# An audio tower with routed experts on one core: streams laid out time by time, layer 4 in three blocks, and expert tiles ordered and cut by their tokens

## What is computed

```python
CONVS = [(128, 10, 5)] + [(128, 3, 2)] * 4 + [(128, 2, 2)] * 2
for w, g, b, s in zip(conv_ws, ln_gs, ln_bs, strides):
    h = gelu(layernorm_over_channels(conv1d(h, w, s), g, b))
out = layernorm(h) @ proj_w + proj_b                 # (64, 12, 192)
attn = softmax(q @ k.T * SCALE) @ v                  # 6 heads of 32, 12 tokens
route_prob = softmax(xt @ Ws + bs)                   # 768 tokens, 9 experts
p, routes = max(route_prob), argmax(route_prob)
h = gelu(xt @ W1[e] + b1[e]); out_e = h @ W2[e] + b2[e]   # 192 -> 768 -> 192
final = where(routes == 0, common * scaling, p * out_routes + (1 - p) * common)
```

## Time and profile before

| | |
|---|---|
| median of 3 runs | 563.9 us (563.47 to 564.89) |
| the profiled execution | 564.41 us, of which the page's span is 562.6 us |
| PE / PEld busy | 537.1 us (95%) / 504.7 us (90%) |
| ACT / DVE / POOL busy | 322.7 (57%) / 309.5 (55%) / 258.6 us (46%) |
| mean granted TensorE clock | 0.982 |

### The profile page before, as it was taken

One profiled execution on the slowest core, in us unless ns is written; L12 is line 12 of the kernel. 1 busy time (PEld: TensorE's weight loads), 2 busy tenths in 40 slices (PEclk: granted clock), 3 DMA queues, 4 the chain that ended last, 5 costly groups with the idle time before them and its releaser, 6 DMA issues.

```text
span 562.6 us, 11208 instructions
## 1 busy us (share of the span) xinstructions
PE 537.1 (95%) x4099; PEld 504.7 (90%) x4099; DVE 309.5 (55%) x767; ACT 322.7 (57%) x557; POOL 258.6 (46%) x298
## 2 busy tenths in 40 slices
PE   6898999999999999999999999999999997899995
PEld 6797989999999999999999999999899886799995
DVE  4665465457567666757575766654564443612231
ACT  1567657747675776677575757773663423444440
POOL 5683464785239427732863394243242120033343
PEclk9999999999999999999999999999999996799998
DMA  7490001692000100000000000000000087151110
GB/s 196 124 276 10 1 15 35 171 239 59 20 1 20 24 5 7 20 22 5 2 20 20 7 20 1 20 6 2 2 6 6 0 218 193 40 142 44 45 39 12
DMA packets 19505, 29.46 MB, mean 52 GB/s; under 512 B 2620, under 2 KB 13846, under 8 KB 19452
## 3 DMA queue, kind: packets, MB, share of 16 engines
q1 hardware_dynamic: 16140, 18.95, 12.7%
q0 software_dynamic: 3296, 9.78, 6.9%
q10 hardware_dynamic: 16, 0.00, 0.0%
HBM read 17.09 MB, written 9.18 MB: 47 GB/s over the span
## 4 chain that ended last, share of the span: by engine, by line
PE 88%; ACT 3%; POOL 2%; DVE 2%; issue 2%; DMA 0%; SPq 0%; POOLq 0%; DVEq 0%; ACTq 0%
PE ps L805 23%; PE ps L797 11%; PE ps L794 8%; PE ps L824 7%; PE ps L1076 5%; PE ps L878 4%; PE ps L1065 3%; PE ps L1064 3%; PE ps L899 3%; PE ps L799 2%; PE ps L795 2%; PE ps L944 2%; PE ps L967 2%; PE ps L887 2%; PE ps L888 1%
## 5 line engine op out<-in xcount | busy, mean ns | idle before, releaser
L649 POOL TENSOR_TENSOR rstd<-ssum,neghalf 128x4 f32<-128x4 f32 (+8 forms) x128 | 116.3, 908 | 195.8 <-DVE ssum L1180 195.4
L805 PE MATMUL ps<-wt,wide 128*124 128x128 f32 (+3 forms) x1248 | 149.5, 274 | 2.5 <-ACT wide L1517 2.1
L805 PEld LDWEIGHTS ps<-wt,wide 128*124 128x124 f32 (+3 forms) x1248 | 142.7, 180 | 5.5 <-issue 2.8
L1486 ACT ACTIVATE work<-ps 128x512 f32<-128x512 f32 (+8 forms) x128 | 66.3, 518 | 131.9 <-PE ps L805 73.0
L1189 DVE TENSOR_TENSOR work<-ps,rstd 128x512 f32<-128x512 f32 (+8 forms) x128 | 75.3, 588 | 75.4 <-POOL rstd L649 71.6
L1180 DVE TENSOR_REDUCE ssum<-work 128x4 f32<-128x516 f32 (+8 forms) x128 | 74.8, 584 | 57.3 <-ACT work L1486 56.9
L643 POOL TENSOR_TENSOR rstd<-var,half 128x12 f32<-128x12 f32 (+3 forms) x39 | 79.0, 2039 | 7.8 <-DVE var L1117 7.2
L1528 ACT ACTIVATE h<-ps,lncol 128x512 f32<-128x512 f32 (+1 forms) x120 | 79.7, 712 | 1.8 <-PE ps L878 1.8
L1503 ACT ACTIVATE wide<-ps,lncol 128x256 f32<-128x256 f32 (+1 forms) x112 | 74.1, 770 | 2.2 <-PE ps L824 2.1
L797 PE MATMUL ps<-wt,h 128*128 128x256 f32 x288 | 70.1, 380 | 0.0
L824 PE MATMUL ps<-ident,work 128*128 128x128 f32 (+3 forms) x416 | 64.8, 268 | 1.2 <-ACT wide L1503 0.8
(11 more groups left out here) (239 smaller groups left out, 825.5 us busy)
## 6 DMA issues: line engine op xcount, KB each, us to landing
sorted_tokens<-zero POOLq DMA_DIRECT2D x1, 5886.5 KB, 30.4
W2s<-in_L_ffn_W_dram SPq DMA_DIRECT2D x9, 576.0 KB, 8.4
wide<-in_L_ffn_W_dram SPq DMA_DIRECT2D x8, 576.0 KB
cols<-cols SPq DMA_DIRECT2D x24, 128.0 KB, 2.2
cols<-sorted_tokens SPq DMA_DIRECT2D x13, 96.5 KB, 1.9
xnat<-in_x_dram SPq DMA_DIRECT2D x7, 130.0 KB, 2.1
wt<-in_L_ffn_b_dram SPq DMA_DIRECT2D x1, 864.0 KB, 5.0
wide<-in_L_tok_conv_w_dram SPq DMA_DIRECT2D x4, 192.0 KB, 3.1
```

The source lines that it names most:

```text
L649: gp.tensor_tensor(rstd[0:rows, idx, 0:count], ssum[0:rows, idx, 0:count], neghalf[0:rows, 0:count], ALU.pow).then_inc(rstd_done, 1)
L805: last = nc.tensor.matmul(y[0:rows, j * C:(j + 1) * C], h[l - 1][g % 2][:, at:at + rows], wt[:, TAP0[l] + tap, :], start=(tap == 0), stop= ...
L1486: nc.scalar.activation(sq[0:rows, n % 2, 0:CUTS[l][k], 0:C], ybank(n)[0:rows, 0:w].rearrange("p (j c) -> p j c", c=C), ACT.Square).then_in ...
```

## The change

It does the following:

- Positions of a group now run time by time: all eight streams of a time stand together. The x loads, layer 1's transposition and GELU patterns and the `h` reads follow. Padding positions between streams fall away, so that block rows become 120, 112, 128, 96, 96 and layer 4 needs three blocks, not four. Layer 2 is cut 4, 4, 2, 3.
- HEAD, BODY, RUN_0 and RUN_1 are written anew; LAST, DRAIN, RUN_5 to RUN_7 stay.
- An expert tile is one of 48 pieces (8 experts by 6 pieces of 128 rows). DVE works out in 8 instructions on 48 partitions how full each piece is and how many are fuller; two small PE matmuls inside `AFTER` turn that into the owners and rows of the 13 fullest, and `owners()` copies them. Tile j works on `WIDTH[j]` tokens: 128 for the first six, then 109, 96, 85, 76, 69, 64 and 59.
- Fewer memsets of padding, and a cleared `sorted_tokens` of 6912 rows, not 7808.

```diff
-ROWS = (NE - 1) * REGION + NTILE * P
+ROWS = NE * REGION
+PIECES = (NE - 1) * REGION // P
+WIDTH = [min(P, TOKENS // (j + 1)) for j in range(NTILE)]
-ROWS_OF = [P, P, 124, 116, 100, 100, 104]
+ROWS_OF = [P, P, 120, 112, P, 96, 96]
-CUTS = [None, (4, 4, 4, 4, 4, 4, 1), (4, 3, 3, 3), (4, 3), (4,), (2,), (1,)]
+CUTS = [None, (4, 4, 4, 4, 4, 4, 1), (4, 4, 2, 3), (4, 3), (3,), (2,), (1,)]
...
-RUN_1 = {'turn_h': 3, 'stat_h': 3, 'power_h': 4, 'project': 5, 'stat_1': 5, 'power_1': 4, ...
+RUN_1 = {'turn_h': 4, 'stat_h': 3, 'power_h': 4, 'project': 5, 'stat_1': 5, 'power_1': 5, ...
...
-                        at = (EVEN[l - 1] if tap == 1 else tap // 2) + rows * (lo + j)
+                        at = (EVEN[l - 1] if tap == 1 else BT * (tap // 2)) + rows * (lo + j)
...
-                        at = tr[:, d * P + i * 64:d * P + i * 64 + 1]
-                        to = bass.AP(at.tensor, at.offset, [at.ap[0], [1, P // 2], [P if d else 3 * P, 2]])
+                        at = tr[:, d * P + i * BT:d * P + i * BT + 1]
+                        to = bass.AP(at.tensor, at.offset, [at.ap[0], [2 * BT, SEG // 2], [P if d else 3 * P, 2], [1, BT]])
...
-                        to = bass.AP(at.tensor, at.offset, [at.ap[0], [shift, v.stop - v.start], [1, w], [LEN1, P // 2]])
+                        to = bass.AP(at.tensor, at.offset, [at.ap[0], [BT * shift, v.stop - v.start], [BT * LEN1, SEG // 2], [1, w * BT]])
                         last = nc.scalar.activation(to, src, ACT.Gelu, bias=lncol[:, 9:10], scale=lncol[:, 1:2])
...
+                if n == FIND_AT:
+                    pe.wait_ge(s_steps, 1)
+                    pe.wait_ge(s_placed, 1)
+                    for v in range(2):
+                        last = nc.tensor.matmul(pa[0:1, 32 + v * NTILE:32 + (v + 1) * NTILE], owner[:, v:v + 1], placed[:, :],
+                                                start=True, stop=True)
+                    last.then_inc(s_which, 1)
...
-                    o = ps[:, 2 * b + f // 4, (f % 4) * P:(f % 4 + 1) * P]
-                    nc.tensor.matmul(o, w[0:DH, 0, f * P:(f + 1) * P], xst[0:DH, b, 0, :], start=True, stop=False)
+                    o = ps[:, 2 * b + f // 4, (f % 4) * P:(f % 4) * P + WIDTH[j]]
+                    nc.tensor.matmul(o, w[0:DH, 0, f * P:(f + 1) * P], xst[0:DH, b, 0, 0:WIDTH[j]], start=True, stop=False)
...
-                    last = nc.tensor.matmul(o, ht[:, b, f * P:(f + 1) * P],
+                    last = nc.tensor.matmul(o, ht[:, b, f * P:f * P + WIDTH[j]],
```

More of the change, by code:

```diff
@@ L74, in needed @@
     ends = [ROWS_OF[layer - 1] * sum(CUTS[layer - 1][:i + 1]) for i in range(len(CUTS[layer - 1]))]
-    return next((i for i, e in enumerate(ends) if e > 2 * rows), len(ends) - 1)
+    return next((i for i, e in enumerate(ends) if e >= 2 * rows + BT), len(ends) - 1)
 def first_block(layer, k):
@@ L230 @@
 AFTER = [('down', 6), ('up', 3, 0), ('up', 3, 1), ('up', 3, 2), ('up', 3, 3), ('up', 3, 4), ('up', 3, 5), ('down', 7)]
+FIND_AT = 2
 LAG = 2
@@ new lines @@
+RUN_1 = {'turn_h': 4, 'stat_h': 3, 'power_h': 4, 'project': 5, 'stat_1': 5, 'power_1': 5, 'norm_1': 6, 'turn_1': 7, 'copy_1': 7, 'qkv': 8, 'split_queries': 8, 'split_keys': 8, 'scores': 9, 'mask': 9, 'less_max': 9, 'exp': 9, 'sum_probs': 9, 'turn_probs': 10, 'copy_probs': 10, 'values': 11, 'divide': 11, 'turn_heads': 13, 'copy_heads': 13, 'out_project': 15, 'residual': 15, 'power_2': 15, 'norm_2': 16, 'turn_2': 17, 'copy_2': 17, 'logits': 18, 'choose': 18, 'rank': 21, 'slot': 22, 'scatter': 26}
@@ L321, in audio_tower @@
         ring = h0[:, :].rearrange("p (r l m) -> p r l m", r=RING, l=BLK)
-        wide = sb("wide", [P, 2 * DFF + 2 * sum(ODD[l] + EVEN[l] for l in range(1, 6))])
+        wide = sb("wide", [P, max(2 * DFF * NE, 2 * DFF + 2 * sum(ODD[l] + EVEN[l] for l in range(1, 6)))])
         W1s = wide[0:DH + 1, 0:2 * DFF * NE].rearrange("p (e k c) -> p e k c", e=NE, k=2)
@@ L418, in audio_tower @@
         onesm = sb("onesm", [M, M])
[L419 to L422, removed]
-        tiles3 = sb("tiles3", [1, NE, TOKENS // P])
-        tiles = sb("tiles", [1, NE])
-        base3 = sb("base3", [1, NE, NE])
-        upto = sb("upto", [1, NE])
-        skip = sb("skip", [1, NE])
-        own3 = prod[0:1, 0:NTILE * NE].rearrange("p (j e) -> p j e", j=NTILE)
-        skip3 = prod[0:1, NTILE * NE:2 * NTILE * NE].rearrange("p (j e) -> p j e", j=NTILE)
-        ownf = sb("ownf", [1, NTILE])
-        owni = sb("owni", [1, NTILE], I32)
-        rowf = sb("rowf", [1, NTILE])
-        rowi = sb("rowi", [1, NTILE], I32)
+        lack = sb("lack", [PIECES, NE - 1, REGION // P])
+        tie = sb("tie", [PIECES, PIECES])
+        steps = sb("steps", [PIECES, NE - 1])
+        owner = sb("owner", [PIECES, 2])
+        jcol = sb("jcol", [PIECES, NTILE])
+        key = sb("key", [PIECES, PIECES])
+        key3 = key[:, :].rearrange("p (e m) -> p e m", e=NE - 1)
+        mine = sb("mine", [PIECES, PIECES])
+        fuller = sb("fuller", [PIECES, 2])
+        placed = sb("placed", [PIECES, NTILE])
+        which = sb("which", [1, 2, NTILE], I32)
+        owni, rowi = which[:, 0, :], which[:, 1, :]
         slotf = sb("slotf", [M, NT])
@@ L781, in conv @@
                     pe.wait_ge(xh_done, n - 2)
-                if chunk == (2, 1, 0):
-                    pe.wait_ge(s_pad, 10)
                 if l == 1:
@@ L1389, in over @@
                 return x.unsqueeze(2).to_broadcast([M, NT, n])
-            count = pa[0:1, 16:16 + NE]
-            chain(nc.vector.tensor_tensor(tiles3[:, :, :], count.unsqueeze(2).to_broadcast([1, NE, TOKENS // P]), full[:, :, :], ALU.is_gt))
-            chain(nc.vector.reduce_sum(tiles[:, :], tiles3[:, :, :], axis=X))
-            chain(nc.vector.tensor_tensor(base3[:, :, :], below[:, :, :], tiles[:, :].unsqueeze(1).to_broadcast([1, NE, NE]), ALU.mult))
-            chain(nc.vector.reduce_sum(upto[:, :], base3[:, :, :], axis=X))
@@ L1403, in _ @@
[L1403 to L1407 removed]
+            count = pa[0:PIECES, 17:16 + NE]
@@ new lines, in _ @@
+            chain(nc.vector.tensor_tensor(key3, count.unsqueeze(2).to_broadcast([PIECES, NE - 1, REGION // P]), lack[:, :, :], ALU.add))
+            chain(nc.vector.tensor_scalar(key[:, :], key[:, :], 0.0, float(P), ALU.max, ALU.min))
+            chain(nc.vector.scalar_tensor_tensor(out=key[:, :], in0=key[:, :], scalar=64.0, in1=tie[:, :], op0=ALU.mult, op1=ALU.add))
+            chain(nc.vector.tensor_tensor(mine[:, :], key[:, :], ident[0:PIECES, 0:PIECES], ALU.mult))
+            chain(nc.vector.reduce_sum(fuller[:, 0:1], mine[:, :], axis=X))
@@ new lines, in _, with owners @@
+            chain(nc.vector.tensor_scalar(mine[:, :], key[:, :], fuller[:, 0:1], None, ALU.is_gt))
+            chain(nc.vector.reduce_sum(fuller[:, 1:2], mine[:, :], axis=X))
+            nc.vector.tensor_scalar(placed[:, :], jcol[:, :], fuller[:, 1:2], None, ALU.is_equal).then_inc(s_placed, 1)
+            def owners():
+                ve.wait_ge(s_which, 1)
+                nc.vector.tensor_copy(which[:, :, :], pa[0:1, 32:32 + 2 * NTILE].rearrange("p (v j) -> p v j", v=2)).then_inc(s_own, 1)
```

125 lines of the change are left out of this document (56 added, 69 removed), and 64 rows, old and new, of tables (BODY, HEAD).

## The result

The changed kernel takes 555.85 us (median of 5, 554.55 to 559.54) against 563.54 us of the kernel before, run beside it (563.21 to 564.89): a ratio of 0.9862, 95% interval 0.9838 to 0.9887, or 7.7 us less. The forecast was 556.5, 7.4 us less.

What follows compares the result with a forecast made beforehand. PE was taken to bound the bodies, busy 51.78 of 51.78 us. Layer 4 and transposes -6.0, tile transposes -0.5, finding +0.3, head -1.2 make -7.4: from 563.9 to 556.5 us, 8-in-10 range 552.8 to 560.8.

Steps and rivals of the forecast that it cites:

- Layer 4 in three blocks: Layer 4 on PE in 8 groups: 48 passes of 0.109 us go, 5.2 us less.
- Transposes of all layers: PE transposes: 0.2 us less in layer 4, 0.6 us less in layers 2, 3, 5 and 6.
- GELU of layer 1: ACT, layer 1: 820 ns falls to at most 660, perhaps 560; off the path in bodies, felt in the head.
- Head: From 20 to 140 us, where PE waits for ACT: 1.2 us gained; ends 3.75 gained and 2 lost.
- Expert tiles: Seven of 13 tiles narrower by 338 columns: 0 in `up_tile` and `down_tile`, 0.5 us less in tile transposes.
- rival 2: `up_tile`: pass cost follows moving columns below 96 too, 6.4 us gained, time 550.1 us; chance 7%.
- Routing and finding: Eight DVE instructions take 1.8 to 3.7 us, PE waits little; four short PE passes add 0.3 us.
- Bodies and order: `turn_h` and `power_1` one slot later in each body: taken as 0; other end 3 us lost in five bodies.
- rival 1: Waits of the new order eat part: head gains nothing, `stat_h` costs 2 to 3 us; 560.0 us; chance 15%.
- The end: Last group's attention and routing, partly at 1.2 GHz: prediction is wrong if the granted clock there changes much; no size given.

Runs made afterwards that it cites:

- spare GELUs: Changed kernel with an unread GELU of 64 elements ahead of each layer-1 GELU: 559.54 us, ratio 0.9923 to the kernel before.
- old order: Changed kernel with HEAD, BODY, RUN_0 and RUN_1 as before the change: 562.37 us, ratio 0.9978 to the kernel before.
- spare matmuls: Changed kernel with seven unread matmuls of 128 to 512 columns behind six serving steps of the last group: 552.85 us, against 555.85.
- the four built on it: Kernel of 552.85 us with all expert tiles 128 wide (551.64 us), widths rounded to 16 (553.24), head filled with unread matmuls (551.99), or wide tiles plus head fill (550.83).
- rounded kernels: Expert tile widths rounded up to multiples of 16, on the changed kernel (555.43 us) and on the one with late unread matmuls (553.24 us).

## Why the prediction was right, and where it was not

The total was right to 0.7 us, within the range, and faster by more than 0.3% as forecast. Layer 4 and the head came as forecast; several smaller terms did not, and their errors had opposite signs, so that the total is closer than the working. That is luck.

**Layer 4 in three blocks** (-5.2): right; undoing it costs 5.3 us by the medians and 5.1 by the bodies.

**Transposes of all layers** (-0.8, of which 0.2 in layer 4): not tested alone, and not seen. Two transposes of fewer columns do start closer together, as forecast (0.088 us at 100 columns, 0.110 at 128, in the kernel before). But all transposes of a body take 4.69 us where they took 4.70, and 0.1 less was forecast. What takes up the difference stays open.

**GELU of layer 1** ("In the bodies that is off the path"): 562 ns instead of 820 was the price foreseen. That it is off the path does not hold in the new order, where spare GELUs cost 0.25 us a body; but the gain of the bodies is not where they cost. The reading behind the step, that PE busy for 51.78 of 51.78 us waits for nothing, was false: the body of before held waits of 0.2 to 0.3 us under the record of the pass ahead. (The forecast also counts 25 chunks of layer 1 a group; there are 25 blocks in 7 chunks. No term uses it.)

**Head** (-1.2): 1.30 us came, from (1,0,1) to group 2 (67.45 to 66.15), for two reasons. With short GELUs and the old order it is 66.70, with spare GELUs and the new order 67.01. So the shorter GELU is worth 0.7 to 0.9 us there and the new order 0.4 to 0.6, by which of them is taken first.

**Expert tiles** (0 for `up_tile`, -0.5 for their transposes): the first right, down to 59 moving columns, which ends rival 2 (a pass's cost following its moving columns). The second did not come: two transposes start 0.064 us apart at 69 columns, not 0.109, but the loop takes 63.98 us against 63.97 before; and the last store cost 0.7 more, for which the forecast had nothing. The Trainium skill ("TensorE: Matmul & The Clock Gate", section "LDWEIGHTS (loading the stationary operand)") has the load take as long as its stationary columns ask; the 0.22 us for two passes at 59 columns agree. By its gap for an isolated pass (section "Back-to-back issue gap") they would have halved; they did not shrink, and that section itself says that in a stream of loads and matmuls both set the distance.

**Routing and finding** (+0.3): 1.87 us on DVE, the lower of the two prices; PE did not wait for `placed`, and `owners()` left 5.0 us of cover. No cost on the path.

**Bodies and order** (0): this is the term that was wrong. Beyond layer 4 a body gained 0.42 us, 2.1 in five, at the layer-0 products and the transposes of the raw samples, and that went with the old order. I weighed only `stat_h` against `turn_h`; there DVE waits 0.56 us and nothing follows from it (read from the trace, no run moved it alone). Nowhere did I ask what lies beside the two table loads once layer 2 is cut 4, 4, 2, 3: with the old tables 0.69 us a body is lost there, 3.4 of the 6.5 us that the old order costs. The form of rival 1 (a wait of the new layout eats the gain) was right for a kernel whose tables stay, at 562.4 us.

**The sum by what was measured:** -5.1 (layer 4) - 2.1 (the rest of five bodies) - 1.3 (head) - 0.5 (the last groups, beyond layer 4: from one `turn_h` to the next 32.96 to 32.02, then 36.24 to 35.35 us) + 0.7 (last store) = -8.3, against -7.7. The 0.6 between them are not placed; the stretch behind the last `turn_h`, in which the half clock lies, went from 34.6 to 37.4 us in the profiles without spare matmuls.

**The end:** the forecast said that it fails if the clock there changes much. It does so from one execution to the next: executions of one and the same kernel lie up to 5 us apart, and that is more than most terms. That the median was little moved by it is luck too.

## What to carry to other kernels

An engine that is busy for the whole of a stretch may still wait: compare the distances of starts of like instructions, kind by kind, and look at the waits of PEld beside those of PE. Loading the neighbour engine shows what its speed is worth in the new order, not what it was worth in the old one. When blocks or chunks change size, list what each one covered on other engines, table loads first, and move the step rather than the chunk. Where the end of a kernel has short waits on TensorE, spare matmuls in them can be worth more than half of what taking out 48 passes was. Look at the granted clock of every execution all the same: one kernel with them ran within 1.5 us, the four built on it within 2.3 to 4.3.

## What the runs showed that was not expected

- A float32 pass with 128 stationary columns takes 0.11 us at 128, 109, 96 and down to 59 moving columns; narrowing the moving side alone brought nothing.
- An indirect store took POOL 0.98 to 1.04 us at 128 rows, 0.97 at 96, 0.96 at 64, but 2.38 us at 109 and 1.66 at 59. With 64 rows in the last tile, in the rounded kernels, it was 0.92.
- The granted clock fell to half (1.2 GHz) behind or in waits of 0.94 and 2.35 us at the end, for 13.7 to 20.5 us in the profiled executions without spare matmuls; in some executions also in the head, at 17 to 20 us, for 3.4 to 6.8 us. Spare work in the late waits brought the mean clock from 0.985 to 0.995 and took 3.0 us off, but with longest waits of 0.5 and 0.6 us the clock still fell for 10.2 us in one profiled execution.
- Waits of 0.2 to 0.3 us stood in a stretch in which PE counts as busy without a gap.
